# Front attention of a two-part kernel: values as weights in four column groups, turned output, unpadded keys, new orders

## What is computed

```
qkv = y @ W_qkv + b_qkv                       # q, k, v: 16 heads of 16 features, 256 tokens
sim = -(q_row_2 - 2.0 * qk + k_col_2) / denom # three numbers per head from the sizes of q, k and y
x1  = x + (softmax(sim) @ v) @ W_proj + b_proj
kx  = modulated_linear(x1, cond)              # then attention of the heads of a token among themselves
x2  = modulated_linear(softmax(kx kx^T / 4) @ kx, cond)
x   = x1 + layers(x2)                         # 6 x (local attention, gated feed-forward)
```

## Time and profile before

| | us |
|---|---|
| three runs | 3410.66, 3404.22, 3412.95 |
| their median | 3410.66 |
| the profiled execution | 3411.51 |
| its span in the profile | 3410.2 |
| front, from the start to the end of its barrier | 682.5 |
| layers and output, the rest of the span | 2727.7 |

### The profile page before, as it was taken

The page is one execution under the profiler, slowest core; times in us unless marked ns, Lnnn a source line. Parts: engine busy times, 40 slices in busy tenths (PEclk is TensorE's granted clock), DMA queues, the critical chain, the costliest instruction groups (busy, mean ns, idle before and its releaser), DMA issues. The chain is left out here.

```text
span 3410.2 us, 81590 instructions
## 1 busy us (share of the span) xinstructions
PE 3224.1 (95%) x30608; PEld 2897.2 (85%) x30608; DVE 2761.9 (81%) x5003; ACT 2537.3 (74%) x7087; POOL 1926.9 (57%) x1536
## 2 busy tenths in 40 slices
PE   4899999469999999999999999999999999999997
PEld 3788888358999898998989989989898999889996
DVE  2247877778888998889988899888998889998883
ACT  1667877258787787777887878878788877887784
POOL 4326654555565656565655566565656566565651
PEclk7889898589999999999999999999999999999999
DMA  3111100011000010001100010000000000100000
GB/s 123 56 32 35 32 32 7 4 56 37 2 2 11 26 44 2 2 2 36 35 11 2 2 36 25 21 2 2 20 31 29 2 2 12 39 29 8 5 8 25
DMA packets 27781, 75.35 MB, mean 22 GB/s; under 512 B 4120, under 2 KB 9848, under 8 KB 27128
## 3 DMA queue, kind: packets, MB, share of 16 engines
q1 hardware_dynamic: 22224, 52.89, 4.9%
q0 software_dynamic: 4864, 16.78, 1.6%
q10 hardware_dynamic: 304, 0.47, 0.1%
HBM read 65.94 MB, written 4.19 MB: 21 GB/s over the span
## 5 line engine op out<-in xcount | busy, mean ns | idle before, releaser
L1542 POOL TENSOR_TENSOR turned<-by_cos,turned 128x512 f32<-128x512 f32 x384 | 493.4, 1285 | 990.3 <-DVE turned L1992 990.3
L1800 ACT ACTIVATE prob<-ps_s,ebias,rnorm 128x128 f32<-128x128 f32 x1536 | 683.9, 460 | 13.7 <-DVE ebias L2012 11.6
L1546 POOL TENSOR_TENSOR rnorm<-norm,half 128x8 f32<-128x8 f32 x384 | 645.5, 1681 | 41.0
L1809 ACT ACTIVATE prob_t<-ps_t 128x512 f32<-128x512 f32 x384 | 230.5, 600 | 313.5 <-PE ps_t L1632 308.9
L1986 DVE TENSOR_TENSOR by_cos<-ps_qk,cos_t 128x512 f32<-128x512 f32 x384 | 264.9, 690 | 122.2 <-ACT sq L1773 119.2
L1569 PE MATMUL ps_qk<-w_hi,x_hi 128*128 128x512 f32 x768 | 328.9, 428 | 18.7 <-DVE x_lo L1976 14.0
L1708 PE MATMUL ps_f<-hid_hi,w_hi 128*128 128x256 f32 (+1 forms) x1056 | 318.0, 301 | 8.6 <-DVE hid_lo L2066 8.2
L2005 DVE TENSOR_REDUCE negmax<-ps_s 128x8 f32<-128x1024 f32 x192 | 234.0, 1219 | 107.7 <-PE ps_s L1623 107.6
L2000 DVE TENSOR_SCALAR norm<-norm 128x8 f32<-128x8 f32 x384 | 309.3, 805 | 13.2
L1800 ACT ACTIVATION_READ_ACCUMULATOR prob<-ps_s,ebias,rnorm 128x1 f32 x1536 | 316.8, 206 | 0.0
L1569 PE MATMUL ps_qk<-w_hi,x_lo 128*128 128x512 f32 x768 | 305.1, 397 | 0.0
(11 more groups left out here) (280 smaller groups left out, 10301.0 us busy)
## 6 DMA issues: line engine op xcount, KB each, us to landing
w_raw<-in_w_qkv SPq DMA_DIRECT2D x24, 768.0 KB, 4.8
w_raw<-in_w SPq DMA_DIRECT2D x12, 693.0 KB, 4.0
w_raw<-in_w_o SPq DMA_DIRECT2D x12, 512.0 KB, 3.7
w_raw<-in_w SPq DMA_DIRECT2D x6, 768.0 KB, 4.3
x_tok<-in_x SPq DMA_DIRECT2D x8, 256.0 KB
kept<-x_t SPq DMA_DIRECT2D x8, 256.0 KB, 2.0
w_raw<-kept SPq DMA_DIRECT2D x8, 256.0 KB, 2.9
out<-rows_out SPq DMA_DIRECT2D x8, 256.0 KB, 3.1
```

The costliest lines, as they stand in the source:

```text
L1542: G.tensor_tensor(turned[:, k, :], by_cos[:, :], turned[:, k, :], ALU.add).then_inc(s["turned"], 1)
L1546: G.tensor_tensor(rnorm[:, i % RR, :], norm2[:, k, :], half[:, :], ALU.pow).then_inc(s["rnorm"], 1)
L1800: last = A.activation(prob[:, k, h, :], half_bank(h % 2, k)[:, T(h // 2)], ACT.Exp, bias=ebias[:, i // NU % 2, k, h:h + 1], scale=rnorm[:, ...
```

## The change

It touches only the front and the layout of its inputs (and the contents of the unread half of the last tile of w_2).

- **Weighing.** `weigh(k)` works for two pairs at once (a quad, k = 0 to 31, on PE every second step). The weights are now the values: each head's 16 values stand in a slot of 32 columns (even heads in the first half, odd heads in the second, the rest zero), and the transposed probabilities of 256 tokens move. The four heads of a quad write to four groups of 32 partitions of OB; the quad of odd heads adds to that of even heads. OB then holds the output turned, with features on the partitions.
- **Heads by parity.** `head(j, e)` says which head a slot of q holds: a quad has four heads of one parity.
- **Turned output.** `flip_o` goes. The inverse sums are spread over 16 columns a head (`widen`, ACT), transposed (`inv_rows`, PE), copied (`inv_rows`, ACT), and `attention_out` multiplies OB by them straight into o_t.
- **Keys.** k_t has two tiles of 128 in place of four, without padding; q keeps slots of 32 partitions and is zero where the other head lies. `slots(q, 1, 1)`, its matmuls and its evictions go; `k_sizes` has two sums fewer and sorts them with a new mask `own`.
- **Buffers.** pr_t keeps two pairs whole (by j % 2) in place of the two halves of one, v_rows grows by two and is cleared once by DVE.
- **Orders.** All five loops over t are new, with 161 steps: on PE scores at 71 (55 before), transposes at 73 (57), weighing at 75 (58), project_out at 82 (66), heads_out at 101 (85); on ACT softmax at 75 and the copies at 76 (55 and 56), with q_sizes at 72, k_sizes at 74, mixer_silu at 68, flip_y at 70, the head exponentials at 91 and 94, widen at 83; on DVE softmax at 73 (55), sum_inverse at 82, attention_out at 83; on POOL gather at 60 (41). BANK0 and BANK1 are shifted alike.

```diff
-    m["w_qk"] = sb("w_qk", [P, KT, 2 * FQ])
+    m["w_qk"] = sb("w_qk", [P, KT, FQ + D])
...
-    m["q_t"], m["k_t"] = sb("q_t", [P, 2, NTILE, N]), sb("k_t", [P, 2, NTILE, N])
-    m["v"] = sb("v_rows", [P, 2, NU, D])
+    m["q_t"], m["k_t"] = sb("q_t", [P, 2, NTILE, N]), sb("k_t", [P, 2, KT, N])
+    m["v"] = sb("v_rows", [P, 2, NU, NH * SLOT])
...
-    m["pr"], m["pr_t"] = sb("pr", [P, 2, 2, NU, N]), sb("pr_t", [P, NU, 2, NU, P])
+    m["pr"], m["pr_t"] = sb("pr", [P, 2, 2, NU, N]), sb("pr_t", [P, 2, 2, NU, N])
     m["psm"], m["pri"] = sb("psm", [P, 2, NU, NH]), sb("pri", [P, NU, NH])
-    m["o"], m["o_t"] = sb("o", [P, NU, D]), sb("o_t", [P, KT, N])
+    m["inv"], m["o_t"] = sb("inv", [P, KT, N]), sb("o_t", [P, KT, N])
...
-FRONT_STEPS = 142
+FRONT_STEPS = 161
...
                 E.wait_ge(s["q"], 2 * b + 2)
-                E.wait_ge(s["k"], 2 * b + 2)
+                E.wait_ge(s["k"], b + 1)
...
-                    last = E.matmul(SB[:, 2 * (j % 2) + e, u * N:(u + 1) * N], q_t[r, b % 2, t, T(u)], k_t[r, b % 2, t, :],
+                    last = E.matmul(SB[:, 2 * (j % 2) + e, u * N:(u + 1) * N], q_t[r, b % 2, t, T(u)], k_t[r, b % 2, t // 2, :],
...
-        def weigh(j, u):
-            b, hp = divmod(j, HP)
-            E.wait_ge(s["prt"], 2 * j + u + 1)
-            if hp == 0 and u == 0:
+        def weigh(k):
+
+            b, t = divmod(k, HP // 2)
+            half, odd = divmod(t, 2)
+            E.wait_ge(s["prt"], 4 * k + 4)
+            if t == 0:
                 E.wait_ge(s["v"], b + 1)
                 if b:
-                    E.wait_ge(s["o"], b)
-            for e in range(2):
-                h = 2 * hp + e
-                for c in range(NU):
-                    last = E.matmul(OB[:, u * D + h * HD:][:, 0:HD], pr_t[:, u, e, c, :],
-                                    v[:, b % 2, c, h * HD:(h + 1) * HD], start=c == 0, stop=c == NU - 1)
+                    E.wait_ge(s["o_t"], b)
+            for c in range(NU):
+                for g in range(4):
+                    h, r = 8 * half + 2 * g + odd, slice(SLOT * g, SLOT * g + SLOT)
+                    last = E.matmul(OB[r, half * N:(half + 1) * N], v[:, b % 2, c, h * SLOT:(h + 1) * SLOT],
+                                    pr_t[:, g // 2, g % 2, c, :], start=odd + c == 0, stop=odd == 1 and c == NU - 1,
+                                    skip_group_check=True)
             last.then_inc(s["av"], 1)
 
-        def flip_o(b):
-            E.wait_ge(s["o"], b + 1)
-            after(BANK0, "flip_o", b)
-            flip(o, M0).then_inc(s["oflip"], 1)
+        def inv_rows(b):
+            E.wait_ge(s["wide"], b + 1)
+            after(BANK0, "inv_rows", b)
+            for half in range(2):
+                for u in range(NU):
+                    last = E.transpose(M0[:, half * N + u * P:][:, 0:P], m["wide"][:, u, T(half)], ident[:, :])
+            last.then_inc(s["inv_ps"], 1)
...
             A.wait_ge(s["prt_ps"], 2 * j + u + 1)
-            if j:
-                A.wait_ge(s["av"], 2 * j + u - 1)
-            A.activation(pr_t[:, u, :, :, :].rearrange("p a b c -> p (a b c)"), PB[:, :], ACT.Copy).then_inc(s["prt"], 1)
-
-        def flip_o(b):
-            A.wait_ge(s["oflip"], b + 1)
+            if j >= 2:
+                A.wait_ge(s["av"], j // 2)
+            A.activation(pr_t[:, j % 2, :, :, T(u)].rearrange("p e c n -> p (e c) n"),
+                         PB[:, :].rearrange("p (a n) -> p a n", n=P), ACT.Copy).then_inc(s["prt"], 1)
+
+        def widen(b):
+            A.wait_ge(s["pri"], b + 1)
             if b:
-                A.wait_ge(s["x1_ps"], b)
-            A.activation(o_t.ap(), two(M0), ACT.Copy).then_inc(s["o_t"], 1)
+                A.wait_ge(s["inv_ps"], b)
+            A.activation(m["wide"].ap().rearrange("p u (h d) -> p (u h) d", d=HD),
+                         m["pri"].ap().rearrange("p u h -> p (u h)").unsqueeze(2).broadcast_to([P, NU * NH, HD]), ACT.Copy
+                         ).then_inc(s["wide"], 1)
+
+        def inv_rows(b):
+            A.wait_ge(s["inv_ps"], b + 1)
+            if b:
+                A.wait_ge(s["o_t"], b)
+            A.activation(inv.ap(), two(M0), ACT.Copy).then_inc(s["inv"], 1)
...
-                V.wait_ge(s["av"], 2 * HP * (a - 1))
-            V.tensor_tensor(v[:, a % 2, :, :], two(M1), row(1), ALU.add).then_inc(s["v"], 1)
+                V.wait_ge(s["av"], HP // 2 * (a - 1))
+            for u in range(NU):
+                slot = v[:, a % 2, u, :].rearrange("p (m y d) -> p m y d", y=4, d=HD)[:, :, ::3, :]
+                by_head = [r.rearrange("p (m y d) -> p m y d", y=2, d=HD) for r in (M1[:, u * D:(u + 1) * D], m["rows"][:, 1, :])]
+                last = V.tensor_tensor(slot, by_head[0], by_head[1], ALU.add)
+            last.then_inc(s["v"], 1)
...
         def sum_inverse(b):
             V.wait_ge(s["exp"], HP * b + HP)
+            if b:
+                V.wait_ge(s["wide"], b)
             V.reciprocal(pri.ap(), psm[:, b % 2, :, :]).then_inc(s["pri"], 1)
 
         def attention_out(b):
-            V.wait_ge(s["pri"], b + 1)
-            V.wait_ge(s["av"], 2 * HP * (b + 1))
+            V.wait_ge(s["inv"], b + 1)
+            V.wait_ge(s["av"], HP // 2 * (b + 1))
             if b:
-                V.wait_ge(s["oflip"], b)
-            V.tensor_tensor(o.ap().rearrange("p u (h d) -> p u h d", d=HD), two(OB).rearrange("p u (h d) -> p u h d", d=HD),
-                            pri.ap().unsqueeze(3).broadcast_to([P, NU, NH, HD]), ALU.mult).then_inc(s["o"], 1)
+                V.wait_ge(s["x1_ps"], b)
+            V.tensor_tensor(o_t.ap(), two(OB), inv.ap(), ALU.mult).then_inc(s["o_t"], 1)
...
-    def slotted(w):
-
-        z = np.zeros((w.shape[0], NH, SLOT), w.dtype)
-        z[:, :, :HD] = w.reshape(w.shape[0], NH, HD)
-        return z.reshape(w.shape[0], NH * SLOT)
+    def by_quad(w):
+        z = np.zeros((w.shape[0], 2, 2, 4, 2, HD), w.dtype)
+        heads = w.reshape(w.shape[0], 2, 4, 2, HD)
+        for odd in range(2):
+            z[:, :, odd, :, odd] = heads[:, :, :, odd]
+        return z.reshape(w.shape[0], FQ)
...
-            for j in pairs(t, 58):
-                weigh(j, 0)
...
-            for j in pairs(t, 57):
-                flip_p(j, 0)
...
-            for j in pairs(t, 55):
-                scores(j)
...
+            for j in pairs(t, 73):
+                flip_p(j, 0)
...
+            for k in quads(t, 75):
+                weigh(k)
...
+            for j in pairs(t, 71):
+                scores(j)
...
+            for j in pairs(t, 73):
+                flip_p(j, 1)
```

More of the change, by code:

```diff
@@ L667, in pe @@
[L667 to L680 removed]
+                flip_y(q)
+            for _ in once(t, 9):
+                net_out(_)
@@ new lines, in act @@
+            for q in batches(t, 71):
+                slots(q, 0, 0)
+            for q in batches(t, 104):
+                heads_out(q)
+            for q in batches(t, 66):
+                flip_x(q)
+            for j in pairs(t, 76):
+                flip_p(j, 0)
+            for q in batches(t, 84):
+                inv_rows(q)
+            for j in pairs(t, 75):
+                softmax(j)
+            for q in batches(t, 71):
+                slots(q, 0, 1)
+            for _ in once(t, 53):
+                mix_exp(_)
```

548 lines of the change are left out of this document (268 added, 280 removed).

## The result

The changed kernel takes 3372.4 us, median of four runs (3370.5 to 3374.6), against 3410.5 us for the kernel before in the same session: 0.9892 of it, 95% interval 0.9879 to 0.9904, some 37 us less. The forecast was 3356, with a range of 3315 to 3398. The profiled execution of after took 3374.6 us, its span is 3373.1.

What follows compares the result with a forecast made beforehand. PE's own work was taken to bound the front's middle part. Savings of 20 (first two batches), 24 (four with gathers), 4 (undisturbed), 6 (last) and 1 (pipe end, first keys) made 55 us: 3411 to 3356, range 3315 to 3398.

Steps and rivals of the forecast that it cites:

- The weigh call: PE, weighing: four column groups overlap, 1.1 us a call, 4.4 us a batch, 9.2 less than now.
- rival 3: PE, weighing: full-height column groups stream one after another, only the keys' saving remains, 3396 us; chance 0.05.
- PE stops being the bound: Undisturbed batch: PE's work falls from 58.4 to 47.5 us, ACT comes to 52.2 with its wait, batch about 54.5.
- rival 1: All eight batches: PE-bound throughout, so everything gives, 97 us less, 3314 us; chance 0.10.
- The first two batches: Start of the middle part, without heads: stay bound by PE, 10 us less each, 20 in all.
- The gathers: Four batches with gathers: the stand in the gather stays, the low-clock loss shrinks, 6 us less each, 24 in all.
- The new wait: ACT's copy of even pairs waits for weighing of earlier pairs: under 1 us a batch, 4.4 if uncovered.
- Rival 2: Middle batches: the new wait isn't covered and DVE's maxima come late, 3 to 4 us a batch remain, 3382; chance 0.13.
- Rival 4: New orders take the gain back: inv_rows on PE waits for widen on ACT, DVE's reciprocal queues, 3408 us; chance 0.05.
- Rival 5: PE's clock: gaps bring 1.2 GHz more often, mean below 0.77 makes batches longer, 3425 to 3460 us; chance 0.07.
- The first weighing: First weigh call, at 122.4 us in before: a shift of more than 5 us would make the prediction wrong.
- The tail and the layers: After the last weighing: the tail's 66.5 us stay, and the layers' part moves by no more than 5 us.

Runs made afterwards that it cites:

- e4: The kernel after with the two loops of a weigh call exchanged, so each column group's two matmuls come one after the other: 3369.1 us, 0.9869 of before.
- e6: The kernel after with more PE work alone: three of a batch's four weigh calls run their records twice more first: 3386.9 us, 0.9917 of before.
- e1: The kernel after with the power for the scales (scale_root) moved ahead of the gathers in POOL's list: 3345.0 us, 0.9799 of before.
- e2: The kernel before with the power for the scales moved ahead of the gathers in POOL's list: 3388.2 us, 0.9919 of before.
- e12: The kernel of e2 run once more for a second profile: 3399.9 us, 0.9967 of before.
- e8: The kernel after with the orders of DVE's and POOL's lists taken from before: 3396.3 us, 0.9945 of before.
- e9: The kernel before with the orders of DVE's and POOL's lists taken from after: 3479.0 us, 1.0185 of before.
- e7: The kernel of e1 with POOL's head output product cut to 16 columns, leaving part of the computation out: 3307.7 us, 0.9691 of before.
- e3: The kernel after with three buffers of a pair's transposed probabilities instead of two: 3367.7 us, 0.9863 of before.
- e5: The kernel after with the edits of both e1 and e3: 3341.0 us, 0.9781 of before.

## Why the prediction was right, and where it was wrong

The direction and the range held, and 3372.4 us lies in the likeliest band, 3335 to 3375, near its upper end; of the 55 us foreseen 37 came. The end of the front, a sign of its own, was foreseen at 627 us and came at 646.8. Point by point:

**The weigh call.** 1.1 us foreseen, 1.00 measured to the next start in 16 of the 25 calls between 200 and 570 us; three at the low clock take 1.86, and in the others PE stood behind the call for another engine. Column groups of full height run four at a time, which rival 3 doubted; in e4 the order of issue changes the call by 0.02 us. The Trainium skill, TensorEngine Tiling (Array Packing), Tiling Modes, has a drain of TensorE at each change of the mode; whatever it takes here is inside this 1.00.

**PE stops being the bound.** Right: e6 shows that 26 us more work on it in five batches cost 0.6, so rival 1 has nothing for it in the middle. The sum for PE was too low all the same: it is busy for 50.9 of 56.3 us in the undisturbed batch, 47.5 of 54.5 foreseen. The call isn't the reason, being cheaper than foreseen; the mean clock of 0.98 gives about 1 us of the 3.4, and the rest isn't taken apart.

**The first two batches.** -20 foreseen, -23.7 measured; e6 confirms that PE still counts there. So it does in the last batch, -6 foreseen and -8.4 measured.

**The gathers.** This is the step that failed, and with 22 of the missing 18 us it is more than the whole miss. The prediction said "the stand in the gather stays, the loss at the low clock shrinks, since PE has slack: 6 each". The reading behind it, that all engines stand while the gathers move 306 GB/s, took two things that happen at the same time for cause and effect: e1 has the traffic without the stop. The gathers are six issues on POOL, and behind them in the same in-order queue stands an operation of 0.6 us that the whole next batch waits for. In before DVE waited for it for 5.8 us in three batches and PE for 2.5, and the simplest reading is that PE's other work covered the rest. The change took much of that work away (10.9 us a batch by the prediction), and added the turning of the keys ahead of the power (1.0 us), so the same queue showed as 22.7 and 18.5 us in three. The stand didn't stay as it was, it took the gain. e1 gives it back, 29 us in these four batches, where e2 and e12 find 3. The prediction had said of gathers only that they stand "as before" in the queue: it had costed what moves, and not what stands behind a thing that doesn't move.

**DVE.** 46.1 us foreseen for the undisturbed batch, 51.5 measured. Its work hardly changed; its products of the heads went from 62 to 83 us over the front since they now meet POOL's, and one product of 1024 columns more falls into this batch. e8 and e9 put this on the orders: the four groups of products sum to 61.1 us in after with the old orders and to 81.7 in before with the new ones. The price for the missing 1.8 us of the undisturbed batch (56.3 against 54.5) is probably of this kind: e7 without POOL's products has 54.1, but it has the power first and a shorter POOL list too.

**ACT.** 48.4 foreseen, 48.2 measured; its wait for the mixer 3.0 us where 3.8 was kept. Its share is 86%, under the 88 that was named as a sign.

**The new wait.** "Under 1 us a batch": 0.9 us of idle time ahead of the copies in the undisturbed batch, 0.4 of them for the weighing, and e3 and e5 give 0.3 to 1 a batch. Right in the middle, though the wait sums to 15.9 us over the front. Rival 2, 3382 us, came nearer than the forecast did, but with this wait as its first cause, and that isn't where the time went.

**The orders.** Rival 4 had them take the gain back. For the orders of DVE and POOL the opposite is true (e8): they carry half of the gain or more. Rival 4's own chain, the inverse sums by way of ACT and PE, was tested by no run. The prediction called it near zero for the pace. In after it is what DVE waits for longest in the undisturbed batch, most of DVE's 4.8 us of idle time:

```profile
DVE o_t L1197 <- ACT inv L882: 3.8, 1, 3.8
```

Over the eight batches this wait is 36.8 us; in before DVE stood 38.1 us ahead of the same product, mostly for the weighing. So the change put one wait in place of another, and what the new one costs stays open. The sum of the prediction had no term for the orders at all. Without the new ones of DVE and POOL the new work gives 11 to 19 us, not 55, so part of the closeness of the forecast is luck.

**The clock.** Mean 0.89 to 0.98 in the middle, far from 0.77. Rival 5 didn't come. e9 is the nearest thing to it, a kernel that new waits on PE make slower, and a good third of what they cost in the batch shown is clock.

**The first weighing** moved by 6.3 us (122.4 to 128.7), past the bound of 5 that I gave. This is no delay of the work: a call now needs two pairs, and it stands behind the first transposes of a third, which start at 127.6 us; before began the last call of its second pair at 133.3 us, after is through with both at 130.5.

**The tail and the layers** stay, as said (67.0 us, and 2726.3 against 2727.7).

## What to carry to other kernels

When an engine that bounds a stretch gets faster, what stands in the other engines' in-order queues ahead of what it waits for decides how much of the gain is seen: go through each such queue and ask when the small operation comes that everybody waits for, also where the change doesn't touch it. A transfer that coincides with a stop isn't shown to be its cause; look for the same traffic without the stop. And a hand-made order is fitted to its durations, so judge orders and work together. Here the new orders alone cost 63 us and the new work alone gave 11 to 19, and both together gave 37.

## What the runs showed of the hardware

Four column groups of 128 rows and 32 columns, streaming 256 columns each, run at the same time: 16 records in 1.00 us to the next start, where one after the other would be 3.5 (16 times the 0.216 us of project_v's records), with sets of four starting within 20 ns. Grouping the matmuls by column group (e4) changes the call by 0.02 us.

DVE's elementwise operations on SBUF stood until a product of POOL beside them had ended: a product of two inputs went from 0.95 to 3.07 us beside a POOL operation of 2.33, a scaling with one input from 0.40 to 1.77, a product of 16 columns from 0.17 to 2.04. DVE's reductions aren't held up: 1.21 us beside a product of POOL (the one at 384.55 us in after) and 1.21 without it (e7).

The granted clock went to 0.50, that is 1.2 GHz, in a stop of PE of 2.1 us (e9) and stayed there for over 16 us of unbroken work; after a stop of 3.8 us in the same batch it was back at 1.00 in less than 4 us. In before it fell at 552 us without any stop. How long the low clock lasts isn't told by the length of the stop here, and the price of a short wait in a stretch that PE bounds is uncertain by as much: in e9's batch 7.8 us of waits came with 6 us more at the low clock than before has.
